# Softmax attention over 16 heads: how value products, score products and row maxima follow each other

## The reference

```python
q = apply_rope((x @ Wq.T + bq)...)      # 2 batches, 16 heads of 8, 1024 tokens each
k = apply_rope((x @ Wk.T + bk)...)
v = (x @ Wv.T + bv)...
scores = einsum('bhsd,bhed->bhse', q, k) * scale
attn = softmax(scores, axis=-1)
out = einsum('bhse,bhed->bhsd', attn, v) ... @ Wo.T + bo
```

## Time and profile before

| | us |
|---|---|
| median of 3 runs | 886.65 (886.46 to 887.20) |
| the profiled execution | 887.39 |
| its span | 886.1 |
| TensorE products, busy | 735.5 |
| VectorE, busy | 668.5 |
| ScalarE, busy | 513.5 |
| GpSimd, busy | 237.5 |
| reductions L1034, 256 | 300.9 busy, 23.7 idle before them |
| exponentials L1173, 512 | 265.9 busy, 53.8 idle before them |

### The profile page before, as it was taken

The page is one execution under the profiler, slowest core; times in us unless marked ns, Lnnn a source line. Parts: engine busy times, 40 slices in busy tenths (PEclk is TensorE's granted clock), DMA queues, the critical chain, the costliest instruction groups (busy, mean ns, idle before and its releaser), DMA issues. The chain is left out here.

```text
span 886.1 us, 18667 instructions
## 1 busy us (share of the span) xinstructions
PE 735.5 (83%) x7088; PEld 359.6 (41%) x7088; DVE 668.5 (75%) x1333; ACT 513.5 (58%) x1012; POOL 237.5 (27%) x295
## 2 busy tenths in 40 slices
PE   6999968888529999909887999999999999956880
PEld 2333246644319999905111222222222222235870
DVE  7878975456875555557886999999999998955555
ACT  3744422564524444454346888888888888943453
POOL 0130010314027766351751200000000000006763
PEclk9999989985758999968658999999999999976995
DMA  3430000000173112133876040404130000023113
GB/s 98 108 85 3 1 23 5 4 3 0 56 281 124 51 47 50 29 104 87 233 155 192 2 86 2 85 3 86 24 64 1 3 2 2 11 88 114 52 48 98
DMA packets 40912, 55.56 MB, mean 63 GB/s; under 512 B 12328, under 2 KB 27824, under 8 KB 40440
## 3 DMA queue, kind: packets, MB, share of 16 engines
q1 hardware_dynamic: 36856, 46.24, 19.6%
q0 software_dynamic: 3968, 8.13, 3.4%
HBM read 35.41 MB, written 14.75 MB: 57 GB/s over the span
## 5 line engine op out<-in xcount | busy, mean ns | idle before, releaser
L1034 DVE TENSOR_REDUCE arena<-psum 128x1 f32<-128x1024 f32 x256 | 300.9, 1217 | 23.7 <-PE psum L918 20.9
L1173 ACT ACTIVATE arena<-psum 128x512 f32<-128x512 f32 x512 | 265.9, 605 | 53.8 <-PE psum L937 53.7
L918 PE MATMUL psum<-arena 56*128 56x512 bf16 x512 | 180.7, 413 | 10.6 <-DVE arena L1034 8.9
L937 PE MATMUL psum<-arena 59*128 59x512 bf16 x512 | 156.2, 389 | 5.5 <-ACT arena L1173 3.6
L948 PE MATMUL psum<-arena 128*32 128x512 f32 x1024 | 138.1, 611 | 8.7 <-issue 8.7
L369 PE MATMUL psum<-arena 128*128 128x128 f32 x808 | 109.5, 284 | 0.4 <-DVE arena L420 0.4
L937 PEld LDWEIGHTS psum<-arena 59*128 59x128 bf16 x512 | 38.4, 94 | 166.0 <-ACT arena L1173 141.2
L369 PEld LDWEIGHTS psum<-arena 128*128 128x128 f32 x808 | 103.4, 200 | 0.7 <-DVE arena L420 0.7
L485 POOL DMA_INDIRECT rows_y<-arena x62 | 61.7, 994 | 38.8 <-DVE arena L434 33.0
L1242 POOL TENSOR_SCALAR arena<-arena 128x16 f32<-128x16 f32 x16 | 4.1, 254 | 249.4 <-DVE arena L1034 249.2
L396 PE MATMUL psum<-arena 128*128 (+1 forms) x496 | 67.5, 280 | 2.4 <-ACT arena L464 1.9
(11 more groups left out here) (312 smaller groups left out, 1056.2 us busy)
## 6 DMA issues: line engine op xcount, KB each, us to landing
arena<-scr_k SPq DMA_DIRECT2D x15, 448.0 KB
arena<-scr_q SPq DMA_DIRECT2D x15, 448.0 KB
arena<-in_f_up SPq DMA_DIRECT2D x1, 4096.0 KB, 14.5
arena<-rows_y SPq DMA_DIRECT2D x12, 256.0 KB, 4.7
scr_q<-arena SPq DMA_DIRECT2D x6, 384.0 KB, 3.3
arena<-in_f_down SPq DMA_DIRECT2D x1, 2048.0 KB, 17.2
arena<-in_f_up SPq DMA_DIRECT2D x1, 2048.0 KB, 9.3
rows_x<-xn SPq DMA_DIRECT2D x5, 256.0 KB, 13.1
```

The costliest lines, as they stand in the source:

```text
L918: mm = pe.matmul(ps[:, bank + half, :], q[rows, k, h, (qh * 4 + qt) * P:(qh * 4 + qt + 1) * P], kk[rows, k, h, half * BLK:(half + 1) * BLK ...
L937: pe.matmul(ps[:, score_bank(n), :], kk[0:KA, k, h, kb * P:(kb + 1) * P], q[0:KA, k, h, qh * BLK:(qh + 1) * BLK], start=True, stop=True).t ...
L1034: dve.tensor_reduce(mx[:, qh, h * 4 + qt:h * 4 + qt + 1], ps[:, bank:bank + 2, :].rearrange("p a b -> p (a b)"), X, ALU.max).then_inc(S("a ...
L1173: act.activation(pt[:, (u % 3) * HG + h, :], ps[:, score_bank(n), :], ACT.Exp, scale=float(HD) ** -0.5).then_inc(S("a1_exp"), 1)
```

## The change

Six edits:

1. While maxima tiles are left, `values` of unit u - 2 is issued in two halves of 256 columns, one behind each tile of unit u. Later it is whole, as before.
2. The flag that starts a fresh sum in bank 7 is set by the first half only.
3. Each M is issued ahead of its S.
4. VectorE transposes the maxima of row group e behind tile 16e + 17, not 16e + 19.
5. GpSimd's `rotate` no longer ends in `subtract`; the calls stand in the list. The order changes in one place: `split_rows(1)` stands ahead of `subtract(7)`.
6. SyncE sends the second rows (`max_rows(1)`) behind the stores of blocks 4 and 5, not behind those of 4, 5 and 6.

```diff
-    def values(u):
+    def values(u, half=None):
         st, qh, kb = u // U, u % U // NTB, u % NTB
-        if kb == 0:
-            pe.wait_ge(S("a1_va"), st + 1)
-            if u >= NTB:
-                pe.wait_ge(S("a1_o"), u // NTB)
-        pe.wait_ge(S("a1_exp"), u * HG + HG)
+        at = slice(0, BLK) if half is None else slice(half * (BLK // 2), (half + 1) * (BLK // 2))
+        if half != 1:
+            if kb == 0:
+                pe.wait_ge(S("a1_va"), st + 1)
+                if u >= NTB:
+                    pe.wait_ge(S("a1_o"), u // NTB)
+            pe.wait_ge(S("a1_exp"), u * HG + HG)
         for h in range(HG):
-            mm = pe.matmul(ps[32 * h:32 * h + 32, 7, :], va[:, kb, (st % NG) * HG + h, :],
-                           pt[:, (u % 3) * HG + h, :], start=kb == 0, stop=kb == NTB - 1, skip_group_check=True)
-        mm.then_inc(S("a1_pv"), 1)
+            mm = pe.matmul(ps[32 * h:32 * h + 32, 7, at], va[:, kb, (st % NG) * HG + h, :],
+                           pt[:, (u % 3) * HG + h, at], start=kb == 0 and half != 1, stop=kb == NTB - 1, skip_group_check=True)
+        if half != 0:
+            mm.then_inc(S("a1_pv"), 1)
...
         for i, n in enumerate(beside or (None, None)):
-            scores(u, 2 * i)
-            if n is not None:
-                max_half(n, 0)
-            scores(u, 2 * i + 1)
-            if n is not None:
-                max_half(n, 1)
-            if i == 0 and u >= 2:
-                values(u - 2)
+            for half in range(2):
+                if n is not None:
+                    max_half(n, half)
+                scores(u, 2 * i + half)
+            if u >= 2 and (beside or i == 0):
+                values(u - 2, i if beside else None)
...
-        if n >= 19 and (n - 19) % 16 == 0:
-            max_rows((n - 19) // 16)
+        if n >= 17 and (n - 17) % 16 == 0:
+            max_rows((n - 17) // 16)
...
         pool.wait_ge(S("a1_r0"), n + 1)
-        subtract(n)
...
     rotate(4)
+    subtract(4)
...
     rotate(5)
+    subtract(5)
     split_rows(0)
     rotate(6)
+    subtract(6)
     rotate(7)
     split_rows(1)
+    subtract(7)
     split_rows(2)
...
-    for n in range(4, 7):
-        store_all(n)
+    store_all(4)
+    store_all(5)
     max_rows(1)
+    store_all(6)
     store_all(7)
```

## The result

| us | before | changed |
|---|---|---|
| median of the runs | 886.92 (886.46 to 893.38, 4) | 865.46 (862.29 to 867.49, 4) |
| ratio | | 0.9738 (0.9682 to 0.9795) |
| the profiled execution | 887.39 | 862.29 |
| ahead of the first maxima product | 422.7 | 418.2 |
| from it to the start of the last value product ("the stage") | 355.9 | 335.1 |

The forecast was 866.0, with a range of 861 to 878. So the stage is what I compare from here on: 20.7 us less. Up to S(8,0) it wins 3.1, from S(8,0) to S(16,0) it loses 0.7, from there to S(115,0) it wins 18.0, and 0.4 behind.

What follows compares the result with a forecast made beforehand. A 2.39 us unit chain through TensorE's whole V and ScalarE's exponential was taken as the bound. Loop 17.7 plus start 3.0 made 20.7 us off 887.39: 866.7, or 866.0 as median; range 862 to 870, 861 to 878 reaching to the second case.

Steps and rivals of the forecast that it cites:

- The loop's period of 18.5 us, 17.7 us in all: Main loop: 8 units take 18.5 us, 1.34 less than before; 17.7 us gained from unit 8 to unit 115.
- the wait for bank 7: Once in 8 units, V waits for ScalarE's copy of bank 7: 0.41 us late instead of 0.69, about 0.05 showing.
- A half V of 0.57 and a half unit of 1.11 on TensorE: TensorE in the loop: half a value product takes 0.57 us, half a unit 1.11, just under VectorE's 1.14.
- Maxima ahead of scores: Loop order on TensorE: scores come two by two and find banks free, 0.28 us to spare, leaving only VectorE's 1.14.
- GpSimd's order: Ahead of the loop: group 1's row maxima go before block 7's subtractions, so VectorE's 5.4 us hole goes.
- SyncE's order: Ahead of unit 8: rows behind two store sets, not three; start 4.0 us sooner, worth 3.0 with possible half clock.
- the start: Stretch up to unit 8: forecast to gain 3.0 us, bounds 0 and 5.5.
- TensorE as the limit: Rival in the loop: half a unit costs TensorE 1.18 us, a period 19.3, total 876; chance 0.14.
- Weight loads in the way: Slower rival in the loop: V's doubled loads are exposed, half a unit 1.24 us, total 889; chance 0.04.
- Scores lose their partner: Slower rival in the loop: one score and maxima pair per unit runs in series, period 21.7 us, total 908; chance 0.05.
- only the start moves: Rival: the loop stays at 2.39 us a unit through a missed chain, total 884; chance 0.06.
- its tail: Behind unit 115, after the maxima end: forecast no change, since V is whole there and ScalarE is the limit.

Runs made afterwards that it cites:

- the extra product: Changed kernel plus one float32 product of 64 columns, on zero value columns, behind each half V; slower chip: 908.89 us (1 run), 8 units 19.51 us.
- Quarters: Changed kernel with each half V issued as two quarters of 128 columns: 865.73 us (1 run), 8 units 18.56 us.

## Why the prediction was right, point by point

- *The loop's period of 18.5 us, 17.7 us in all.* Eleven of the twelve periods are 18.38, the last is 18.73, the mean 18.41. VectorE's pitch is 1.131, not 1.14, which takes 0.14 off the sum; the wait for bank 7 puts 0.06 back. The cause was right: halves alone give the period, the extra product shows the 0.02 us of slack on TensorE behind it. The 17.7 us from unit 8 to unit 115 were too small by 1.7: S(8,0) to S(115,0) took 265.8 us and takes 248.5, 17.2 less, with the 2.2 us of the half clock in it, so 19.4 without. Some 1.2 of the 1.7 are the period (1.43 us less, not 1.34), and 0.3 I had taken off for the low clock.
- *A half V of 0.57 and a half unit of 1.11 on TensorE, from two sizes of one form.* Measured 0.57 and 1.11.
- *Maxima ahead of scores.* I worked the pair of edits as one and let the step read as if both were needed. Alone, edit 3 gives nothing, and the halves don't need it.
- *The wait for bank 7, 0.41 late and 0.05 shown.* V's halves come 0.43 late, and the pitches of VectorE behind that (1.186, 1.176 and 1.141 on average) show 0.11.
- *GpSimd's order.* The 5.4 us hole went, as said, and the rows' DMA was the next thing late, as said.
- *SyncE's order: this term was too large.* 3.0 us were put down. S(8,0) comes 3.1 sooner where I had 4.0. The 1.3 us for the rows' own landing stand in no row: each of the four small DMAs took 4.8 to 6.9 us from issue to landing behind the stores, and 2.2 to 2.5 in the kernel before. And the clock did fall, which cost 2.2 us, where I took half of 2.0. With both the start is worth 0.9, which the kernel without edits 4 to 6 confirms (1.0).
- *TensorE as the limit, 876.* It was 0.02 us a half unit away; the extra product is that rival made true.
- *Weight loads in the way, 889.* Quarters, with four times the loads of a whole V, cost VectorE's pitch nothing. Their 16 loads are done in 0.38 us beside products on the same rows, and the passes follow each other at 0.11 us. The Trainium skill's rule in "TensorE: Matmul & The Clock Gate", "Part 3: Packing small matmuls — row/col tiling", that a load overlaps products in flight only where the row group differs, is not borne out for these products in column groups.
- *Scores lose their partner; only the start moves.* The first did not happen in the loop (S and M start within 0.01 us), the second is refuted by the periods.

The mechanism held, but that the sum came out so close is luck, and more of it than the half microsecond at the median shows. The forecast put 20.7 us down to the stage and 20.7 were measured, because two errors cancel: the start was 2.1 us too large (3.0 for 0.9), and the loop 1.7 and its tail 0.4 too small. The kernel with edits 1 to 3 alone shows the loop and its tail by themselves, 19.8 us for the 17.7 of the forecast. And the four runs of the changed kernel lie 5.2 us apart.

## What to carry to other kernels

Where several short instructions wait in a ring of few buffers behind one long one, split the long one so that they come evenly; look for a chain through another engine before believing in the busiest one. Price the pieces by start-to-start times of two sizes of the same form, not by durations. And when a stall on compute goes, look at once at what its DMA stands behind: small transfers that somebody waits for belong ahead of large ones that nobody needs yet. Sending the second rows ahead of the last two sets of stores too was worth 6.2 us here; all edits of the start as chosen, which put the rows ahead of one set only, were worth 1.

## What the runs showed of the hardware

TensorE's granted clock fell to half 3.2 us into the idle time in the kernel before, and about 2.0 us into it in the changed one (mean 0.58 from 472 to 474, idle from 470.4). In the ten profiles with such a stall at units 6 to 8 (nine kernels, the changed one twice) it fell 1.7 to 3.8 us into the idle time, and came back 4.6 to 6.1 us after work resumed (4.8 and 4.9 in those two). The stalls were 2.40 to 6.37 us long, and the clock fell in every one; where the stall lay right ahead of S(8,0), the 8 units behind it took 1.7 to 2.8 us more than a period. So a stall of 2.4 us was not short enough, and what is, no run shows. The two kernels that send the rows ahead of the stores have no stall of TensorE over 1 us there and stay at full clock: that is what they gain besides the stall.

Four products of 128 columns side by side in column groups follow each other at 0.11 us a pass with their loads hidden (V in quarters).

The third chip ran the same kernels 28 to 31 us slower, though the stage of attention took the same time within 0.2 us (335.1 and 335.3). The difference lies in the layers around it: 443.1 us ahead of the stage and not 418.2, 121.9 behind it and not 107.6. I did not look for its cause.
